# The first bias of an expert layer: added by VectorE instead of by a TensorE product, and the expert number read earlier on TensorE

## The chip, the cores and the metric
The kernel runs on one NeuronCore of a Trainium2 chip. The metric is the device time of one launch in microseconds. The engines are called PE (TensorE), DVE (VectorE), ACT (ScalarE), POOL (GpSimd) and SP (SyncE, which here issues DMAs and waits). The times before are three runs: 1462.31, 1463.79 and 1467.72 us.

## What is computed
Cross attention and then a layer of experts, both with a residual, all in fp32 accuracy:

```python
x = x + xattn(layernorm(x), ctx_768, ...)        # 16 x 224 rows of 512, 16 heads, 750 keys
x = x + ffn(layernorm(x), w1, b1, w2, b2, ...)
# ffn: 8 experts of width 256, the 2 best per row by the router, softmax over the 2
h = gelu(einsum('bsd,edh->bseh', x, w1) + b1)    # exact gelu
expert_out = einsum('bseh,ehd->bsed', h, w2) + b2
out = einsum('bse,bsed->bsd', gates, expert_out)
```

The change concerns `b1`, an array of 8 experts x 256 values, and the register that says which expert a tile of rows belongs to.

## The kernel before
The whole work is one program in which each engine has its own list of instructions, written out by hand, with semaphores between them. Matrix products of fp32 accuracy are made of three products of split operands: x = high + low, w = high + low, and high x high + high x low + low x high.

**Attention** is 64 groups (16 batches, 4 groups of 4 heads), pipelined over five groups. `first`, `second`, `third` and `fourth` of each engine give the order inside a group, and `after(g)` and `before(g)` are hooks between groups. The weights of the experts are loaded by SP in 16 pieces of 512 KB (`load_pieces`) during the last groups. A piece is split by ACT (`w_part`, L1007: high) and then DVE (L1400: low = piece - high). ACT splits 11 pieces in its `after(GROUPS)`, DVE four in its own, ahead of the last two residual additions (L1300), for the first of which PE's last output projection (L388 to L390, second row of products) waits.

**Placing.** DVE then chooses the two best experts of each row, computes gates and for each row its place in a list sorted by expert, padded so that every tile of 128 list entries belongs to one expert. There are 63 tiles (`TILES`). The list goes into `table_x` (rows to gather) and `table_t` (rows to add to), and `which_i[i]` is the expert number of tile i.

**The loop over 63 tiles**, which the change touches. For tile i:
- POOL gathers 128 rows of 516 values into `xg` (L801), six tiles ahead, and adds the finished 128x512 tile to `out` by an indirect DMA (L809).
- PE `fold_x`: four transposes (L2110). ACT `x_high` (L1157) and DVE `x_low` (L1666) make high and low parts of it.
- PE `up`: the bias product L2118 (ones, 128x128, times `b1_hl[:, e, :]`, whose row 0 holds the high part of b1, row 1 the low part, and all others zeros), then 12 products with w1 (L2120 to L2122) of 256 columns each, all into one PSUM tile.
- ACT `gelu` (L1164) from that PSUM tile into `hid`.
- PE `fold_h`: two transposes of `hid` (L2130); ACT `h_high` (L1170), DVE `h_low` (L1671).
- PE `down`: six products of 512 columns with w2 (L2139 to L2141).
- DVE `y_bias` (L1682) adds b2 out of `b2_all`, in which the 8 rows of b2 are spread over all partitions; ACT `y_scale` (L1177) multiplies by the gate.

PE's order in turn i is fold_x(i+2), read of the expert number of i+1 (`expert_of`, L2145), up(i+1), down(i), fold_h(i+1). DVE's is x_low(i+2), y_bias(i), read of the number of i+1 (L1676), h_low(i+1). ACT's is x_high(i+2), gelu(i+1), h_high(i+1), y_scale(i). A read is a load of one value out of SBUF into a register of the engine's sequencer, which other instructions of that engine then use in their addresses.

**How b1 gets to its place before.** b1 comes in as 16 rows of 128 values per lane (`b1_s`), PE transposes it into a PSUM bank (L1918, end of group 63), ACT copies the high part (`b1_th`, L1013), DVE the low part (`b1_tl`, L1405). POOL sets `ones_r` to 1 and `b1_hl` to 0 (L732, L733), then SP moves the two parts into rows 0 and 1 of `b1_hl` with two DMAs (L539, L541). The semaphore `b1_both` tells that both have landed. ACT waits for it ahead of its 11 splits, because both parts lie where weights are written later, and PE ahead of the tile loop.

Of the kernel before, what the change touches and what calls it, by code (L numbers as in the profile page):

```python
# [146 lines left out]
def expert_phase(nc, x1_d, w1, b1, w2, b2, centroids, w_route, ident_d, gates_dram, out):  # L147
    x, ctxT, wqT, bq, wkT, bk, wvT, bv, woT, bo, ident, x1 = SCRATCH["attention"]
    with ExitStack() as es:
# [77 lines left out]
        b1_hl, ones_r = in_a("b1_hl", [P, E, DE], F32R), in_a("ones_r", [P, P], F32R)  # L227
# [22 lines left out]
        b1_th, b1_tl = in_q("b1_th", [2 * E, P], F32R), in_q("b1_tl", [2 * E, P], F32R)  # L250
# [75 lines left out]
        b1_hi, b1_both = sem("b1_hi"), sem("b1_both")  # L326
# [18 lines left out]
        ctxv = ctxT.rearrange("b (c p) n -> b c p n", p=P)  # L345

# [53 lines left out]
        with nc.Block() as block:  # L400

            @block.sync
            def _(sp):
# [126 lines left out]
                def before(g):  # L530
# [5 lines left out]
                    if g == GROUPS:  # L536
                        sp.wait_ge(zeroed, 1)
                        sp.wait_ge(b1_hi, 1)
                        sp.dma_start(b1_hl[0:1, :, :].bitcast(F32), b1_th[:, :].bitcast(F32)).then_inc(b1_both, 16)  # L539
                        wait_free(sp, "b1", 0)  # L540
                        sp.dma_start(b1_hl[1:2, :, :].bitcast(F32), b1_tl[:, :].bitcast(F32)).then_inc(b1_both, 16)  # L541
                        sp.wait_ge(s_full, 12 * GROUPS)
                        load_pieces(E + 2, 2 * E)
# [52 lines left out]
                wait_full(sp, "O1", B - 1)  # L596
                sp.dma_start(b2_all[:, :, :], b2.rearrange("(a e) n -> a e n", a=1).broadcast_to([P, E, D])
# [15 lines left out]
            def _(pool):  # L613
# [110 lines left out]
                def constants():  # L724
# [7 lines left out]
                    pool.memset(ones_r[:, :].bitcast(F32), 1.0).then_inc(made, 1)  # L732
                    pool.memset(b1_hl[:, :, :].bitcast(F32), 0.0).then_inc(zeroed, 1)  # L733

                def after(g):
# [13 lines left out]
                    pool.wait_ge(made, 7)  # L749
# [6 lines left out]
                    pool.wait_ge(made, 11)  # L756
# [57 lines left out]
                pool.wait_ge(zeroed, 3)  # L814
# [17 lines left out]
            def _(act):  # L832
# [176 lines left out]
                def after(g):  # L1009
                    if g == GROUPS - 1:  # L1010
                        wait_full(act, "b1", 0)
                        act.wait_ge(x_full, XU * GROUPS)
                        act.activation(b1_th[:, :], bank_of("b1", 0)[0:2 * E, 0:P], ACT.Copy).then_inc(b1_hi, 1)  # L1013
                    if g == GROUPS:
# [4 lines left out]
                        act.wait_ge(b1_both, 32)  # L1019
# [140 lines left out]
                def gelu(i):  # L1160
                    act.wait_ge(h_full, i + 1)
                    if i >= 2:
                        act.wait_ge(ht_full, i - 1)
                    act.activation(hid[:, i % 2, :], HP[:, i % 2, 0:DE], ACT.Gelu).then_inc(gelu_done, 1)  # L1164
# [30 lines left out]
            def _(dve):  # L1195
# [206 lines left out]
                def after(g):  # L1402
                    if g == GROUPS - 1:
                        dve.wait_ge(b1_hi, 1)
                        dve.tensor_tensor(out=b1_tl[:, :], in0=bank_of("b1", 0)[0:2 * E, 0:P], in1=b1_th[:, :],  # L1405
                                          op=ALU.subtract).then_inc(freed("b1", 0), 1)
# [3 lines left out]
                    if g == GROUPS + 2:  # L1410
                        dve.wait_ge(made, 8)
# [106 lines left out]
                dve.wait_ge(made, 5)  # L1518
# [25 lines left out]
                dve.wait_ge(zeroed, 3)  # L1544
# [15 lines left out]
                dve.wait_ge(made, 8)  # L1560
# [50 lines left out]
                dve.wait_ge(made, 12)  # L1611
# [65 lines left out]

                def y_bias(i, e):
# [21 lines left out]
            @block.tensor  # L1700
            def _(pe):
# [447 lines left out]
                pe.wait_ge(b1_both, 32)  # L2149
# [5 lines left out]
                up(0, e)  # L2155
                fold_h(0)
# [53 lines left out]
```

## Time and profile before
| | before |
|---|---|
| median of 3 runs | 1463.79 us |
| the profiled execution: its own time, its span | 1467.88 us, 1466.0 us |
| mean granted TensorE clock in it | 0.976 of full |
| PE busy | 1389.4 us (95%) |
| DVE busy | 970.8 us (66%) |
| ACT busy | 840.8 us (57%) |
| POOL busy | 1082.7 us (74%) |

All views are of the one profiled execution; its own time and its span differ by what lies around the instructions. "Idle before" of a row is the time in which the engine had nothing under way just before that instruction, and behind the arrow stands what ended it. PEld is PE's weight load, which overlaps products. A name with a q (PEldq) is the engine's sequencer: register work and waits, which are not counted as busy. Ends of PE's products are modelled. A chain of waits gives each microsecond to one instruction: to the one that the end of the span was waiting for.

### The profile page before, as it was taken

How to read it: one execution, taken by the hardware profiler on the slowest of the kernel's cores; microseconds unless marked ns; L12 is line 12 of the kernel's file. 1: busy time of each engine (PE TensorE's matmuls, PEld its weight loads, DVE VectorE, ACT ScalarE, POOL GpSimd, SP SyncE). 2: the span in 40 equal slices, each digit the busy share in tenths (PEclk: the TensorE clock that was granted, in tenths of full speed). 3: DMA queues.
4: the chain of work that ended last, by engine and by line, in shares of the span. 5: the costliest groups of instructions: out<-in, count | busy, mean ns of one | idle time of the engine just before them, and what ended most of it. 6: DMA issues, size and time to landing. Idle time of an engine off the chain costs nothing.

```text
span 1466.0 us, 34315 instructions
## 1 busy us (share of the span) xinstructions
PE 1389.4 (95%) x11524; PEld 1109.4 (76%) x11524; DVE 970.8 (66%) x1429; ACT 840.8 (57%) x1825; POOL 1082.7 (74%) x915
## 2 busy tenths in 40 slices
PE   4899999999999999999999999999999767999997
PEld 4777777787777787777777777777786446999986
DVE  6666767677676767677767676767667476444443
ACT  5546565666656566666665656665664552555554
POOL 3468787878787879797978787887877804776775
PEclk9989999999999999999999999999999687999999
DMA  7354545555454555555555554555454763887785
GB/s 242 90 130 109 166 128 154 149 136 156 124 155 123 161 137 140 140 140 139 142 145 154 134 156 124 167 132 152 118 136 125 243 128 75 146 144 131 144 143 85
DMA packets 134952, 206.74 MB, mean 141 GB/s; under 512 B 33808, under 2 KB 70832, under 8 KB 134656
## 3 DMA queue, kind: packets, MB, share of 16 engines
q1 hardware_dynamic: 120544, 173.20, 43.5%
q0 software_dynamic: 14240, 31.35, 11.9%
q8 instruction: 99, 1.62, 0.5%
q14 instruction: 69, 0.57, 0.1%
HBM read 64.29 MB, written 38.66 MB: 70 GB/s over the span
## 4 chain that ended last, share of the span: by engine, by line
PE 87%; DVE 5%; POOL 2%; issue 2%; DMA 2%; SPq 1%; ACT 1%; POOLq 0%; DVEq 0%; ACTq 0%
PE M L388 13%; PE S L1849 12%; PE M L389 12%; PE M L390 12%; PE O L1865 10%; PE M L1826 5%; PE M L2122 2%; PE M L2121 2%; PE M L2120 2%; PE M L2139 2%; PE M L2140 2%; PE M L2141 2%; PE S L2110 2%; PE M L1883 2%; POOL psum_p L634 1%
## 5 line engine op out<-in xcount | busy, mean ns | idle before, releaser
L634 POOL TENSOR_TENSOR psum_p<-psum_p,pr 125x896 f32<-125x896 f32 x254 | 549.8, 2165 | 107.5 <-ACT pr L917 82.1
L917 ACT ACTIVATE pr<-S 125x448 f32<-125x448 f32 x768 | 386.9, 542 | 205.2 <-PE S L1849 196.5
L1257 DVE TENSOR_REDUCE mx_parts<-M 112x2 f32<-112x1024 f32 x256 | 305.6, 1216 | 84.9 <-PE M L1826 84.8
L1849 PE MATMUL S<-qst,kst 128*125 128x224 f32 x1536 | 268.3, 289 | 5.4 <-ACT pr L917 3.2
L1849 PEld LDWEIGHTS S<-qst,kst 128*125 128x125 f32 x1536 | 223.6, 190 | 53.8 <-issue 22.1
L1865 PE MATMUL O<-pr,v 125*32 125x224 f32 x3072 | 185.4, 364 | 0.1
L1261 DVE TENSOR_REDUCE mx_parts<-M 112x4 f32<-112x952 f32 x128 | 141.0, 1143 | 59.6 <-PE M L1826 59.5
L631 POOL TENSOR_TENSOR psum_p<-pr 125x896 f32<-125x896 f32 x64 | 135.5, 2117 | 32.4 <-ACT pr L917 32.3
L388 PE MATMUL M<-ctx_h,wk_h 128*128 128x376 f32 (+1 forms) x384 | 136.2, 355 | 0.6 <-DVE mx_parts L1257 0.5
L389 PE MATMUL M<-ctx_l,wk_h 128*128 128x376 f32 (+1 forms) x384 | 129.9, 338 | 0.0
L885 ACT ACTIVATE kh_s<-M,bk_s 128x376 fp32r<-128x376 f32 (+1 forms) x128 | 73.1, 571 | 98.5 <-PE M L390 95.8
L390 PE MATMUL M<-ctx_h,wk_l 128*128 128x376 f32 (+1 forms) x384 | 129.3, 337 | 0.0
L809 POOL DMA_INDIRECT out<-y_out,table_t x63 | 99.9, 1585 | 39.0 <-ACT y_out L1177 17.9
L801 POOL DMA_INDIRECT xg<-rows_d,table_x x63 | 64.0, 1016 | 85.9 <-DVE settled L1660 45.8
L1865 PEld LDWEIGHTS O<-pr,v 125*32 125x32 f32 x3072 | 86.7, 111 | 53.6 <-issue 15.4
L1277 DVE RECIPROCAL M<-M 128x224 f32<-128x224 f32 x64 | 100.1, 1564 | 38.5 <-PE M L1883 38.3
L388 PE MATMUL M<-wv_h,ctx_h 128*125 128x512 f32 x288 | 117.1, 407 | 0.0
L390 PE MATMUL M<-wv_h,ctx_l 128*125 128x512 f32 x288 | 113.6, 394 | 0.0
L389 PE MATMUL M<-wv_l,ctx_h 128*125 128x512 f32 x288 | 113.5, 394 | 0.0
L1826 PE MATMUL M<-kh_s,q_own 32*112 32x512 f32 (+1 forms) x1024 | 94.4, 399 | 17.0 <-DVE mx_parts L1257 7.7
L1826 PEld LDWEIGHTS M<-kh_s,q_own 32*112 32x112 f32 x1024 | 41.8, 170 | 62.3 <-issue 48.1
L1245 DVE SCALAR_TENSOR_TENSOR kl_s<-M,bk_s,kh_s 128x376 fp32r<-128x376 f32 (+1 forms) x128 | 76.5, 598 | 16.2 <-ACT kh_s L885 15.8
(259 smaller groups left out, 2999.9 us busy)
## 6 DMA issues: line engine op xcount, KB each, us to landing
kst<-kh_s SPq DMA_DIRECT2D x512, 93.8 KB, 2.2
kst<-kl_s SPq DMA_DIRECT2D x256, 93.8 KB, 2.2
ctx_r<-ctxT SPq DMA_DIRECT2D x48, 375.0 KB, 3.7
qst<-qh_s SPq DMA_DIRECT2D x128, 112.0 KB, 3.0
rows_d<-x_res SPq DMA_DIRECT2D x32, 448.0 KB, 4.7
w_l<-w SPq DMA_DIRECT2D x16, 512.0 KB, 7.7
x_ln<-x SPq DMA_DIRECT2D x17, 448.0 KB, 4.6
q_own<-qh_s SPq DMA_DIRECT2D x256, 28.0 KB, 1.8
```

The source lines that it names most:

```text
L388: pe.matmul(out, lhs[0], rhs[0], start=first, stop=False)
L389: pe.matmul(out, lhs[0], rhs[1], start=False, stop=False)
L390: return pe.matmul(out, lhs[1], rhs[0], start=False, stop=last)
L631: pool.tensor_tensor(out=total, in0=tiles[0], in1=tiles[1], op=ALU.add).then_inc(sum_step, 1)
L634: pool.tensor_tensor(out=total, in0=total, in1=tiles[half], op=ALU.add).then_inc(sum_step, 1)
L917: act.activation(pr[0:KP, (3 * g + p) % 2, j, :, :], S[0:KP, n % SB, 0:2 * NQ].rearrange("p (i n) -> p i n", i=2), ACT.Exp).then_inc(exp_d ...
L1257: dve.tensor_reduce(mx_parts[0:QP, pair, u, 0:1], M[0:QP, pair, 0:FIRST_KEYS], AX.X, ALU.max).then_inc(max_done, 1)
L1261: dve.tensor_reduce(mx_parts[0:QP, pair, :, 1], both, AX.X, ALU.max).then_inc(max_done, 1)
L1277: dve.reciprocal(den, den).then_inc(inverted, 1)
L1826: last = pe.matmul(M[0:QP, j, at:at + w], q_own[head, g % 2, QP * qt:QP * (qt + 1)], kh_s[head, g % 2, off:off + w], start=True, stop=True)
L1849: last = pe.matmul(S[0:KP, n % SB, NQ * h:NQ * (h + 1)], kst[:, i, j, o:o + KP], qst[:, i, j, :], start=True, stop=True)
L1865: last = pe.matmul(O[HD * j:HD * (j + 1), 0:NQ], v[0:KP, 2 * p + i, HD * j:HD * (j + 1)], pr[0:KP, (3 * g + p) % 2, j, i, :], start=(p == ...
```

## The change
1. **The bias.** `b1_hl` and `ones_r` go, `b1_all` (128 x 8 x 256, fp32) comes. ACT copies the transposed b1 whole into `b1_t`; SP writes it to DRAM (`b1_rows`, 8 KB, in the place of two DMAs of 8 KB) and reads it back spread over all 128 partitions (`b1_line`, 1 MB) ahead of the load of `b2_all`. POOL's two memsets go, as do DVE's low part, ACT's wait for `b1_both` ahead of its splits and PE's ahead of the loop.
2. **The loop.** PE's product L2118 goes. DVE adds the bias: `h_bias(i)` reads the PSUM tile and `b1_all[:, e, :]` and writes `hid`. The gelu works in place in `hid`. DVE's order in turn i becomes read of the number of i+1, h_bias(i+1), x_low(i+2), y_bias(i), h_low(i+1). up(i) waits for `biased` of i-2 instead of the gelu of i-2.
3. **The read on PE.** The number of tile i+2 is read behind down(i), ahead of fold_h(i+1); before, that of i+1 was read between fold_x(i+2) and up(i+1).

```diff
@@ SP
                     if g == GROUPS:
-                        sp.wait_ge(zeroed, 1)
-                        sp.wait_ge(b1_hi, 1)
-                        sp.dma_start(b1_hl[0:1, :, :].bitcast(F32), b1_th[:, :].bitcast(F32)).then_inc(b1_both, 16)
                         wait_free(sp, "b1", 0)
-                        sp.dma_start(b1_hl[1:2, :, :].bitcast(F32), b1_tl[:, :].bitcast(F32)).then_inc(b1_both, 16)
+                        sp.dma_start(b1_rows, b1_t[:, :]).then_inc(b1_sent, 16)
                         sp.wait_ge(s_full, 12 * GROUPS)
                         load_pieces(E + 2, 2 * E)
...
                 wait_full(sp, "O1", B - 1)
+                sp.wait_ge(b1_sent, 16)
+                sp.dma_start(b1_all[:, :, :].rearrange("p e f -> p (e f)"),
+                             b1_line.broadcast_to([P, E * DE])).then_inc(b1_in, 16)
@@ POOL
-                    pool.memset(ones_r[:, :].bitcast(F32), 1.0).then_inc(made, 1)
-                    pool.memset(b1_hl[:, :, :].bitcast(F32), 0.0).then_inc(zeroed, 1)
@@ ACT
-                        act.activation(b1_th[:, :], bank_of("b1", 0)[0:2 * E, 0:P], ACT.Copy).then_inc(b1_hi, 1)
+                        act.activation(b1_t[:, :], bank_of("b1", 0)[0:2 * E, 0:P], ACT.Copy).then_inc(freed("b1", 0), 1)
...
-                        act.wait_ge(b1_both, 32)
                         for n in range(ACT_EARLY):
                             w_part(n)
...
                 def gelu(i):
-                    act.wait_ge(h_full, i + 1)
-                    if i >= 2:
-                        act.wait_ge(ht_full, i - 1)
-                    act.activation(hid[:, i % 2, :], HP[:, i % 2, 0:DE], ACT.Gelu).then_inc(gelu_done, 1)
+                    act.wait_ge(biased, i + 1)
+                    act.activation(hid[:, i % 2, :], hid[:, i % 2, :], ACT.Gelu).then_inc(gelu_done, 1)
@@ DVE
-                    if g == GROUPS - 1:
-                        dve.wait_ge(b1_hi, 1)
-                        dve.tensor_tensor(out=b1_tl[:, :], in0=bank_of("b1", 0)[0:2 * E, 0:P], in1=b1_th[:, :],
-                                          op=ALU.subtract).then_inc(freed("b1", 0), 1)
...
+                def h_bias(i, e):
+                    dve.wait_ge(h_full, i + 1)
+                    if i >= 2:
+                        dve.wait_ge(ht_full, i - 1)
+                    dve.tensor_tensor(out=hid[:, i % 2, :], in0=HP[:, i % 2, 0:DE], in1=b1_all[:, e, :],
+                                      op=ALU.add).then_inc(biased, 1)
...
                 x_low(0)
                 e = expert_of(0)
                 x_low(1)
+                dve.wait_ge(b1_in, 16)
+                h_bias(0, e)
                 h_low(0)
                 dve.wait_ge(b2_in, 16)
                 for i in range(TILES):
+                    if i + 1 < TILES:
+                        after = expert_of(i + 1)
+                        h_bias(i + 1, after)
                     if i + 2 < TILES:
                         x_low(i + 2)
                     y_bias(i, e)
                     if i + 1 < TILES:
-                        e = expert_of(i + 1)
                         h_low(i + 1)
+                        e = after
@@ PE
                     if i >= 2:
-                        pe.wait_ge(gelu_done, i - 1)
+                        pe.wait_ge(biased, i - 1)
                     h = HP[:, i % 2, 0:DE]
-                    pe.matmul(h, ones_r[:, :], b1_hl[:, e, :], start=True, stop=False)
                     for c in range(DC):
-                        pe.matmul(h, xTs[:, 0, i % 2, c, :], w1_h[:, e, c, :], start=False, stop=False)
+                        pe.matmul(h, xTs[:, 0, i % 2, c, :], w1_h[:, e, c, :], start=c == 0, stop=False)
...
-                pe.wait_ge(b1_both, 32)
...
                 up(0, e)
+                after = expert_of(1)
                 fold_h(0)
                 pe.wait_ge(ew_lo, DVE_LOW)
                 for i in range(TILES):
                     if i + 2 < TILES:
                         fold_x(i + 2)
                     if i + 1 < TILES:
-                        after = expert_of(i + 1)
                         up(i + 1, after)
                     down(i, e)
+                    if i + 2 < TILES:
+                        later_one = expert_of(i + 2)
                     if i + 1 < TILES:
                         fold_h(i + 1)
                         e = after
+                    if i + 2 < TILES:
+                        after = later_one
```

## Rows read from the trace of the kernel before
**Rows 1.** The page's first line: the span of the profiled execution.
```profile
span 1466.0 us, 34315 instructions
```
**Rows 2.** Windows, 1240 to 1440 us: PE, PEld, DVE, ACT, POOL busy, clock, DMA share, GB/s.
```profile
1240.00:1440.00 200.00, 199.73 (x1376) 181.08 (x1375) 98.18 (x166) 108.67 (x221) 139.97 (x109) 1.00 0.77 138
```
**Rows 3.** Chain of waits, 1300 to 1315 us: shares, then start us, us, what.
```profile
by line: PE M L2121 13.6%; PE M L2120 13.5%; PE M L2122 12.9%; PE M L2139 12.5%; PE M L2140 12.4%; PE M L2141 12.4%; PE S L2110 11.6%; PE M L2118 5.7%; PE O L2130 2.9%; PE M L2130 2.9%; issue 0.1%
...
1303.15 0.44 PE S L2110 x4
...
1306.76 0.44 PE S L2110 x4
1307.19 0.12 PE M L2118
```
**Rows 4.** Timeline of PE and PEld in one tile: start us, us, engine, line, operation.
```profile
1308.47 0.29 PE L2122 MATMUL M<-w_h,xTs 128*128 x1
...
1309.75 0.40 PE L2141 MATMUL M<-w_h,hTs 128*128 x1
1309.76 0.37 PEld L2130 LDWEIGHTS O<-id_s,hid 128*128 128x128 f32 x2
1309.99 0.38 PE L2130 MATMUL O<-id_s,hid 128*128 128x128 f32 x2
```
**Rows 5.** Timeline of DVE and ACT in the same tile, idle time before in brackets.
```profile
1307.41 0.72 ACT L1177 ACTIVATE y_out<-y_raw,xg 128x512 f32<-128x512 f32 x1 [0.23 <-DVE y_raw L1682]
1307.62 0.43 DVE L1671 TENSOR_TENSOR hTs<-M,hTs 128x256 fp32r<-128x256 f32 x1 [0.24 <-issue]
...
1308.04 0.58 ACT L1157 ACTIVATE xTs<-S 128x512 fp32r<-128x512 f32 x1
...
1308.65 0.69 DVE L1666 TENSOR_TENSOR xTs<-S,xTs 128x512 fp32r<-128x512 f32 x1 [0.60 <-ACT xTs L1157]
1308.80 0.38 ACT L1164 ACTIVATE hid<-M 128x256 f32<-128x256 f32 x1 [0.18 <-PE M L2122]
...
1310.30 0.69 DVE L1682 TENSOR_TENSOR y_raw<-M,b_all 128x512 f32<-128x512 f32 x1 [0.96 <-PE M L2141]
```
**Rows 6.** Timeline at two places where PE restarts: the first tile, the last.
```profile
1229.32 0.38 ACT L1164 ACTIVATE hid<-M 128x256 f32<-128x256 f32 x1 [1.09 <-PE M L2122]
1229.75 0.29 PEld L2130 LDWEIGHTS O<-id_s,hid 128*128 128x128 f32 x2 [0.77 <-ACT hid L1164]
...
1456.81 0.19 PEld L2139 LDWEIGHTS M<-w_h,hTs 128*128 128x128 f32 x1 [1.35 <-issue]
1456.84 0.47 PE L2139 MATMUL M<-w_h,hTs 128*128 x1 [1.14 <-DVE hTs L1671]
```
**Rows 7.** By source: PE's register read (ns min/median/max), and L2118's idle (us, times).
```profile
L2145 PEldq TENSOR_LOAD <-which_i x63: 298/307/969, 1225.2 to 1451.3; - x63
L2145 PEldq FUSED_REGOPS  x63: 151/151/165, 1225.7 to 1451.8; - x63
...
  issue: 1.7, 6
```
**Rows 8.** Chain of waits and timeline at the start of the expert phase.
```profile
1164.48 4.11 DMA b_hl<-b_tl
...
1166.24 0.34 ACT L946 ACTIVATE lg_parts<-M 128x224 f32<-128x224 f32 x1
1168.77 10.53 ACT L1007 ACTIVATE w_h<-w_l 128x1024 fp32r<-128x1024 f32 x11 [2.20 <-DMA b_hl<-b_tl]
...
1169.86 4.69 DVE L1400 TENSOR_TENSOR w_l<-w_l,w_h 128x1024 fp32r<-128x1024 f32 x4 [1.81 <-ACT w_h L1007]
...
1175.21 0.48 PE L388 MATMUL M<-wo_h,oT_h 128*112 128x512 f32 x1 [2.70 <-DVE x_ln L1300]
```
**Rows 9.** Windows after it, columns as in rows 2.
```profile
1172.80:1176.20 3.40, 0.99 (x4) 0.80 (x5) 3.30 (x5) 3.40 (x4) 0.75 (x2) 1.00 0.89 321
1176.20:1179.60 3.40, 3.40 (x9) 2.12 (x7) 0.88 (x1) 3.10 (x4) 0.00 (x0) 0.50 0.00 0
```

More of the change, by code:

```diff
@@ L226, in expert_phase @@
         w1_h, w1_l = in_a("w1_h", [P, E, DC, DE], F32R), in_a("w1_l", [P, E, DC, DE], F32R)
-        b1_hl, ones_r = in_a("b1_hl", [P, E, DE], F32R), in_a("ones_r", [P, P], F32R)
+        b1_all = in_a("b1_all", [P, E, DE])
         b1_s, lane = in_a("b1_s", [P, 2 * E]), in_a("lane", [P, 1])
@@ L249, in expert_phase @@
         in_q, end_q = region(q_own_at)
-        b1_th, b1_tl = in_q("b1_th", [2 * E, P], F32R), in_q("b1_tl", [2 * E, P], F32R)
+        b1_t = in_q("b1_t", [2 * E, P])
         assert end_q[0] <= q_own_at + 2 * NQ * 4
@@ L325, in expert_phase @@
         made, zeroed, masks = sem("made"), sem("zeroed"), sem("masks")
-        b1_hi, b1_both = sem("b1_hi"), sem("b1_both")
+        b1_sent, b1_in = sem("b1_sent"), sem("b1_in")
+        biased = sem("biased")
         gate_out, need_done, safe = sem("gate_out"), sem("need_done"), sem("safe")
@@ L345, in expert_phase @@
         ctxv = ctxT.rearrange("b (c p) n -> b c p n", p=P)
+        b1_rows = gates_dram.rearrange("a b c -> (a b c)")[0:E * DE].rearrange("(r c) -> r c", c=P)
+        b1_line = gates_dram.rearrange("a b c -> (a b c)")[0:E * DE].rearrange("(a n) -> a n", a=1)
         raw_k = pr[:].rearrange("p a b c n -> p (a b c n)")[:, 0:CC * D]
@@ L748, in after @@
                     pool.memset(going[:, :, :], 1.0).then_inc(made, 1)
-                    pool.wait_ge(made, 7)
+                    pool.wait_ge(made, 6)
                     pool.memset(going[:, :, 0:1], 0.0).then_inc(made, 1)
@@ L755, in after @@
                     pool.tensor_scalar(upper_half[:, :], token[:, :], 0.0, None, ALU.is_ge).then_inc(made, 1)
-                    pool.wait_ge(made, 11)
+                    pool.wait_ge(made, 10)
                     pool.tensor_tensor(out=token16[:, :], in0=token[:, :], in1=upper_half[:, :], op=ALU.add).then_inc(made, 1)
@@ L812, in add_rows @@
                                             oob_is_err=False, compute_op=ALU.add).then_inc(added[i % YO], 16)
-                pool.wait_ge(zeroed, 3)
+                pool.wait_ge(zeroed, 2)
                 for n in range(YO):
@@ L1410, in after @@
                     if g == GROUPS + 2:
-                        dve.wait_ge(made, 8)
+                        dve.wait_ge(made, 7)
                         dve.tensor_scalar(behind[:, :], iota[:, :], float(DUMP + 1), lane[:, 0:1], ALU.add,
@@ L1517, in _ @@
                 gp, g1, g2 = gap[0:QP, :], gate4[0:QP, :, 0, 0], gate4[0:QP, :, 1, 0]
-                dve.wait_ge(made, 5)
+                dve.wait_ge(made, 4)
                 wait_free(dve, "lg", B - 1)
@@ L1543, in _ @@
                 dve.wait_ge(gap_exp, 1)
-                dve.wait_ge(zeroed, 3)
+                dve.wait_ge(zeroed, 2)
                 dve.wait_ge(x1_out, 16 * B)
@@ L1559, in _ @@
                 dve.wait_ge(sums_full, 1)
-                dve.wait_ge(made, 8)
+                dve.wait_ge(made, 7)
                 dve.tensor_tensor_scan(runs.rearrange("p e k -> p (e k)"), going[0:QP].rearrange("p e k -> p (e k)"), sums,
@@ L1609, in find_rows @@
                                       op=ALU.is_equal).then_inc(row_done, 1)
-                dve.wait_ge(made, 12)
+                dve.wait_ge(made, 11)
                 dve.wait_ge(xn_out, 32 * B)
```

## The prediction
> **What bounds the kernel now.** I read the page first, for the span of the profiled execution [rows 1], then the last fifth of it, where the changed loop runs, with the view of windows. From 1240 to 1440 us PE is busy 199.73 of 200 us at full granted clock (2.4 GHz), while DVE works 98, ACT 109 and POOL 140 us [rows 2]. The chain of waits says the same more sharply: over four tiles it consists of PE instructions and 0.1% of "issue", and one tile takes 1306.76 - 1303.15 = 3.61 us [rows 3]. So in this stage every 0.1 us that PE's instruction stream loses or gains in a tile is worth 62 times as much. The stage before it, the start of the expert phase, is a chain through several engines. There I looked for what the old bias path holds up, and found ACT waiting for a DMA of it [rows 8].
>
> **1. The bias product goes.** In the chain L2118 stands with 0.12 us per tile [rows 3]. Its own row would say 0.36 us, but most of that lies under its neighbours. There are 63. The first runs before the loop is filled, at half clock, and is dealt with in step 2. The other 62 give 62 x 0.12 = 7.4 us.
>
> **2. DVE adds the bias between the up products and the gelu.** The nearest row for the new add is the DVE subtraction of the same 128x256 elements, one operand in PSUM: 0.43 us. Its start follows the pattern of y_bias, which has the same two waits and an address from a register: 0.15 us after PE's last product ends (1309.75 + 0.40 = 1310.15, start 1310.30) [rows 4, 5]. Then come a hand-over to ACT of 0.04 us (as x_high ending at 1308.62 and x_low starting at 1308.65), the gelu, 0.38 us, and 0.05 us from the gelu to PE's weight load (1229.70 to 1229.75) [rows 5, 6]. From the end of the up products to the load of fold_h this makes 0.15 + 0.43 + 0.04 + 0.38 + 0.05 = 1.05 us, where today it is 0.04 + 0.38 and then 0.58 us in hand.
>
> The cover is down(i), which lies between them. The up products end at 1308.47 + 0.29 = 1308.76 and the load of fold_h starts at 1309.76, 1.00 us later [rows 4]. That is when PE has it start, not when it must. On a free PE at the end of the kernel a load starts at 1456.81 and its product ends at 1457.31, 0.50 us later for 512 columns. 128 columns take 0.13 us less (0.40 against 0.38 - 0.11 for the first of two), so 0.37 us [rows 4, 6]. fold_h's first product now ends at 1309.99 + 0.27 = 1310.26, so its load could start at 1309.89, 1.13 us after the up products. The bounds for the wait are 0 (1.05 against 1.13) and 0.10 us a tile (1.05 and 0.05 for a slower gelu, against 1.00). I take 0, as the restart on a free PE is the nearest row; the other end costs 62 x 0.10 = 6.2 us.
>
> The gelu now reads SBUF, not PSUM. ACT's 128x512 from SBUF, with a scale from a tensor, takes 0.72 us against 0.58 us from PSUM [rows 5]; part of this is the scale, so 0.05 us is my bound for a slower gelu. The Trainium skill ("VectorE: DVE Perf Modes", "The TRN2 errata") gives ScalarE 224 fixed cycles for an SBUF source and 172 for PSUM; at its 1.2 GHz this would be 0.04 us against the change, still inside the 0.08 us in hand. No row here isolates it.
>
> On DVE, x_low now stands behind the new add: it would start at 1308.76 - 0.12 + 0.15 + 0.43 + 0.03 = 1309.25 and end at 1309.94 [rows 4, 5]. The next up products start about 0.65 us (six transposes of 0.11) behind 1309.64, at 1310.3; 0.35 us are in hand. y_bias, next on DVE, needs it at 1310.18. ACT does nothing new. DVE goes from 1.8 to 2.2 us of work per 3.5 us. For the first tile nothing covers the add: +0.58 us (0.15 + 0.43), against its product at half clock, at least 2 x 0.12 = 0.24 us. I take +0.3 us.
>
> **3. PE reads the expert number earlier.** The register load takes 307 ns in the median and up to 969 ns, followed by 0.15 us of register work; by the program's order the sequencer reaches it only behind fold_h's wait for the gelu. Where it was slow PE stood still ahead of L2118: 1.7 us in 6 tiles [rows 7]. Behind down(i) the read runs beside the up and down products, while the sequencer would wait for the gelu anyway: it has at least the 1.05 us of step 2. At the old place the gelu, 0.58 us later now (0.15 + 0.43 + 0.04, against 0.04), would put the read that much closer to the up products in every tile. Gain 1.7 us; bounds 0 and 1.7.
> Here the Trainium skill speaks against the change: "TensorE: Matmul & The Clock Gate" (Spec table) gives PE a queue of 64, and "Perfetto Trace Analysis" (Tensor Engine Instruction) has the sequencer go on while an instruction waits in the queue. By that rule the read would run far ahead already, and moving it be worth 0. The rows are against it: six stalls of 0.3 us end at L2118 with "issue".
> DVE's read moves the other way, from behind y_bias to behind h_low, where it runs in DVE's idle time ahead of h_full, beside the up products; it costs nothing, and h_low loses a wait.
>
> **4. The old bias path at the start of the expert phase.** ACT is ready for its 11 splits of weights when keep_parts ends, 1166.24 + 0.34 = 1166.58, and stands still for 2.20 us more for the DMA of b1_tl, which lands 4.11 us after its issue. DVE stands still 1.81 us for the first split, then does four of its own until 1174.55, then the residual for which PE waits 2.70 us at 1175.21 [rows 8]. From there on the chain runs through PE, DVE and ACT without a cover to the table and the first gather. Without the wait ACT starts 2.2 us earlier. DVE is free 1.8 us earlier, so the chain gains 1.8 us. Bounds: 0 if another wait stands there, and 1.8 + 1.7. The latter is clock: PE's second row of products, from 1175.21, ran its first microsecond at full (2.4 GHz) and the rest, 3.4 us of it, at half clock (1.2 GHz) [rows 9]; started at 1173.4, most of it would lie in the full stretch and take half of 3.4 us. That stretch is not tied to the kernel, so I take no gain from it, and it can also go against me.
> The added DMAs on SP: 8 KB out, in place of two of 8 KB in, ahead of six weight loads, which can start earlier, as SP no longer waits for POOL's memset; and 1 MB in, ahead of b2 and the gates. At 321 GB/s [rows 9] that is 3.3 us more for the gates. Their cover is DVE's placing of the tokens, from the gates to the table, which the first gather waits for too; without it, 3.3 us. POOL loses two memsets, and nobody waits for what stands behind them.
>
> **Sum.** 7.4 + 1.7 + 1.8 - 0.3 = 10.6 us. In the loop POOL's queue catches up more slowly after each change of expert (its work of 140 / 200 x 3.61 = 2.5 us per tile [rows 2] meets 3.5, not 3.6), for which I take off 0.3 us: 10.3 us. The profiled execution took 1467.9 us (span 1466.0 [rows 1]), 4.1 us above the median of 1463.8; it would come out at 1457.6. The median goes to 1463.8 - 10.3 = **1453.5**, -0.70%. A measurement of this kernel can tell about 0.5% (7.3 us) from no change.
>
> **Rivals.**
> *fold_h waits for the gelu* (20%). If the load must start at its present place, PE waits 0.05 to 0.10 us per tile: 3 to 6 us are given back: 1456.5 to 1459.7. For it: 1.05 us is more than 1.00. Against: the restart row.
> *Slower* (4%). The same place, or x_low behind the add, but much later: it decides from 10.3 / 62 = 0.17 us of wait per tile. With the add as long as y_bias, 0.69 us [rows 5], the chain of step 2 is 1.31 us; against 1.00 us that is 0.31 us a tile, 19.2 us, and 1472.7. Against it: the row of 256 elements is 0.43 us, from PSUM too.
> *The bias path at the start is hidden anyway* (13%): another wait holds ACT or DVE at 1166 to 1169. Then 1453.5 + 1.8 = 1455.3.
> *Reading ahead is worth nothing* (8%): the stalls come from code loading, and stay. Then 1453.5 + 1.7 = 1455.2. The rule on the queue would give this too.
> *Forecast* 55%.
>
> **Numbers.** The range takes in the clock at the start (1.7 us down) and 2 us for the median of few runs; upwards the first rival: 1449 to 1460. Faster by over 0.5% is below 1456.5: the forecast but for 3 points, both small rivals, a fifth of the first: 0.74; same 0.22; slower 0.04.
>
> **What would show it.** L2118's group is gone and the chain's period per tile is 3.49 us; idle before fold_h's load stays near 0 (if it says "<-ACT hid" with 0.05 us or more, the first rival holds); a DVE group hid<-M,b1_all of 63, mean near 425 ns; gelu at 385 to 430 ns. No stall with "issue" ahead of the up products. ACT's first split starts near 1166.6 with no DMA ahead of it, and the first gather near 1217.5. Wrong would be: a period of 3.55 or more, or a first gather that doesn't move.

## The result, and the profile after

The changed kernel takes 1455.45 us in the median of 5 runs (1453.5 to 1458.86), beside 1463.79 us for the kernel before: ratio 0.9939, 95% interval 0.9925 to 0.9952, or 8.3 us less. Two later comparisons, on two different chips, gave 0.9956 and 0.9942. The forecast was 10.3 us less and 1453.5 us. The profiled execution took 1458.86 us, 3.4 us above its median, as the one of before stood 4.1 us above its own.

The page's first lines, of after:
```profile
span 1456.8 us, 34248 instructions
...
PE 1378.8 (95%) x11461; PEld 1100.2 (76%) x11461; DVE 988.9 (68%) x1491; ACT 843.2 (58%) x1825; POOL 1085.0 (74%) x913
```
The same window as in [rows 2], of after (PE, PEld, DVE, ACT, POOL busy, clock, DMA share, GB/s):
```profile
1240.00:1440.00 200.00, 199.47 (x1375) 180.84 (x1374) 117.16 (x230) 114.88 (x229) 146.35 (x114) 1.00 0.79 145
```
PE is as full as it was, and fewer of its instructions are spent on a tile: the chain of waits, 1303 to 1311 us, to be read against [rows 3], has a tile every 3.48 us (1306.99 - 1303.51, 1310.47 - 1306.99) in place of 3.61, with no product of L2118 and no share of "issue".
```profile
1303.51 0.44 PE S L2117 x4
...
1306.99 0.44 PE S L2117 x4
...
1310.47 0.44 PE S L2117 x4
```
One tile's timeline of after, against [rows 4, 5] (idle time before in brackets):
```profile
1308.58 0.28 PE L2128 MATMUL M<-w_h,xTs 128*128 x1
...
1309.00 0.42 DVE L1677 TENSOR_TENSOR hid<-M,b_all 128x256 f32<-128x256 f32 x1 [1.06 <-PE M L2128]
...
1309.34 0.68 DVE L1661 TENSOR_TENSOR xTs<-S,xTs 128x512 fp32r<-128x512 f32 x1
...
1309.46 0.42 ACT L1163 ACTIVATE hid<-hid 128x256 f32<-128x256 f32 x1 [0.60 <-DVE hid L1677]
...
1309.85 0.40 PE L2147 MATMUL M<-w_h,hTs 128*128 x1
1309.93 0.30 PEld L2136 LDWEIGHTS M<-id_s,hid 128*128 128x128 f32 x2
1310.09 0.38 PE L2136 MATMUL M<-id_s,hid 128*128 128x128 f32 x2
```
The up products end at 1308.86, the add starts 0.14 us later, the gelu ends at 1309.88, and the weight load of fold_h starts at 1309.93, 1.07 us behind the up products. That is 0.07 us later than in [rows 4], and yet its product starts 0.24 us behind the last down product, as that one did behind its own predecessor (0.23), so without a gap. The interval of 1.07 us is the same in every tile, to 0.01 us (1.15 in the first), so the load now starts when the gelu is done, and the product when PE is free. The groups by line say it for all 63 tiles (busy us, mean ns, idle time before); fold_h writes to `O` and `M` in turn, so it has two groups:
```profile
L1677 DVE TENSOR_TENSOR hid<-M,b_all 128x256 f32<-128x256 f32 x63 | 26.8, 425 | 68.8 <-PE M L2128 68.8
L1163 ACT ACTIVATE hid<-hid 128x256 f32<-128x256 f32 x63 | 26.4, 419 | 41.4 <-DVE hid L1677 41.4
L2136 PE MATMUL O<-id_s,hid 128*128 128x128 f32 x64 | 12.5, 277 | 1.1 <-ACT hid L1163 1.1
L2136 PE MATMUL M<-id_s,hid 128*128 128x128 f32 x62 | 11.8, 272 | 0.0
```
PE's idle time before fold_h all lies at the first tile (1.15 us in its timeline); in the running loop there is none.

The time between four marks in the two profiled executions, us:
```
                                                before    after
start to the first gather's issue              1219.30  1217.42   -1.9
first gather's issue to the end of fold_x(4)     19.03    20.39   +1.4
end of fold_x(4) to the end of fold_x(62)       210.87   202.61   -8.3
end of fold_x(62) to the end of the span         16.84    16.38   -0.5
```
So the running loop gives the gain, and its start takes some of it back. How much of the first row belongs to the change, the experiments tell.

### The profile page after: what moved, and what is told of

It is laid out like the page before. It is cut to its first block, busy times and chain, and to the rows that moved or that the text cites. A ratio compares the mean times of both kernels' runs of the same rounds, so it can differ in the third digit from the quotient of the medians.

```text
span 1456.8 us, 34248 instructions
## 1 busy us (share of the span) xinstructions
PE 1378.8 (95%) x11461; PEld 1100.2 (76%) x11461; DVE 988.9 (68%) x1491; ACT 843.2 (58%) x1825; POOL 1085.0 (74%) x913
## 4 chain that ended last, share of the span: by engine, by line
PE 84%; DVE 6%; POOL 3%; SPq 2%; issue 2%; DMA 2%; ACT 1%; POOLq 0%; DVEq 0%; ACTq 0%
PE M L392 13%; PE M L393 12%; PE M L394 12%; PE S L1856 12%; PE O L1872 10%; PE M L1833 5%; PE M L2126 2%; PE M L2128 2%; PE M L2127 2%; PE M L2145 2%; PE M L2147 2%; PE M L2146 2%; PE S L2117 2%; PE M L1890 2%; POOL psum_p L638 2%
## 5 line engine op out<-in xcount | busy, mean ns | idle before, releaser
L811 POOL DMA_INDIRECT out<-y_out,table_t x63 | 99.9, 1585 | 38.5 <-ACT y_out L1176 18.7
L803 POOL DMA_INDIRECT xg<-rows_d,table_x x63 | 64.0, 1017 | 74.1 <-DVE settled L1655 40.8
```

## The experiments

Ratios are to the kernel before in the same series, on the same chip; each series had its own chip. The kernel before took 1467.45, 1464.23 and 1464.29 us in the three series.

### First series: the parts one by one

**The bias product put back** (the changed kernel, with one more product a tile; the next one, with start=True, overwrites its result):
```diff
                     for c in range(DC):
+                    pe.matmul(h, xTs[:, 0, i % 2, 0, :], w1_h[:, e, 0, :], start=True, stop=True)
```
(it stands ahead of the loop over c)


> The changed kernel with a 256-column product more at the head of each up, where the bias product stood; the next one starts the sum anew, so its result is not used. If PE's instruction stream is the bound of the loop, the product costs its issue interval, 0.12 us in each of 62 tiles: period 3.60 us, 7.4 us on top of 1455.5, 1462.9. If the loop is by now bound by the chain through DVE and ACT (1.07 us beside the down products), part of it is hidden: the first up products of a tile would start earlier relative to fold_h and the period would stay below 3.55 us, at most +4 us.


Measured: 1465.88 us, ratio 0.9984 (0.9974 to 0.9995). Against the 0.9939 of the whole change, which was measured in another comparison, this is about 6.6 us. The price fits, but the trace had something that neither trace of before and after had. Its timeline at one tile, PE, DVE, ACT and POOL:
```profile
1266.72 1.59 POOL L811 DMA_INDIRECT out<-y_out,table_t  x1 [0.30 <-issue]
...
1267.12 0.28 PE L2129 MATMUL M<-w_h,xTs 128*128 x1
...
1268.43 0.42 DVE L1677 TENSOR_TENSOR hid<-M,b_all 128x256 f32<-128x256 f32 x1 [2.07 <-PE M L2129]
...
1268.89 0.42 ACT L1163 ACTIVATE hid<-hid 128x256 f32<-128x256 f32 x1 [1.61 <-DVE hid L1677]
...
1269.36 0.33 PE L2137 MATMUL M<-id_s,hid 128*128 128x128 f32 x1 [0.57 <-ACT hid L1163]
```
The last up product ends at 1267.40, and DVE starts the add 1.03 us later, where 0.14 us is the rule. The semaphore events of the trace put PE's signal at 1268.30, 0.90 us behind the product's end; DVE's own register read was done by 1267.0. Seven such late signals (0.53 to 0.95 us) stand in this execution, each followed by a tile that took 0.44 to 0.85 us too long; the traces of before and after have none. The trace also shows what ran beside them: all seven products ended while POOL's instruction that adds a finished tile to `out` (L811, 1.59 us) was running, and all seven signals came 0.01 to 0.09 us before its end, here at 1268.30 against 1268.31.

**The read put back** behind fold_h, all else as in the changed kernel:
```diff
                 up(0, e)
-                after = expert_of(1)
                 fold_h(0)
...
+                        after = expert_of(i + 1)
                         up(i + 1, after)
                     down(i, e)
-                    if i + 2 < TILES:
-                        later_one = expert_of(i + 2)
...
-                    if i + 2 < TILES:
-                        after = later_one
```


> The changed kernel with PE's read of the expert number back between fold_x and up. My theory: PE's sequencer does not pass fold_h before the gelu is done (1309.88 in a tile of the changed kernel's trace), the read then takes 0.2 + 0.30 + 0.15 us and the register work for the first address 0.1 us more, so the first up load starts at about 1310.95 instead of 1310.64: 0.3 us of idle time with issue ahead of L2126's load in every tile, and all of the excess of slow reads comes on top. 62 x 0.3 = 19 us and some 4 us for slow reads: 1475 to 1480. The rival (the sequencer runs far ahead of the queue, the read's place is worth nothing): 1455.5, period 3.48 us.


Measured: 1479.38 us (two runs), ratio 1.0075 (1.0051 to 1.0099): 17 to 20 us more than the changed kernel by its three ratios, and slower than the kernel before. The view by source of the first up product's line says where:
```profile
L2126 PEldq FUSED_REGOPS  x252: 46/46/46, 1224.3 to 1466.6; - x126
...
  issue: 24.8, 74
```
(idle time of the weight loads and of the products added up) and the timeline of PEld shows it at three tiles in a row:
```profile
1303.82 0.19 PEld L2126 LDWEIGHTS M<-w_h,xTs 128*128 128x128 f32 x1 [0.25 <-issue]
...
1307.71 0.19 PEld L2126 LDWEIGHTS M<-w_h,xTs 128*128 128x128 f32 x1 [0.37 <-issue]
...
1311.49 0.19 PEld L2126 LDWEIGHTS M<-w_h,xTs 128*128 128x128 f32 x1 [0.27 <-issue]
```
The sequencer's read doesn't get past fold_h while that waits for the gelu: here, as in the kernel before, it starts 0.17 to 0.33 us behind the gelu's end in nearly every tile. The gelu now ends about 0.6 us later, the register load (301 ns in the median here) starts only then, and in these three tiles no weight load runs for 0.25 to 0.37 us; a tile takes 3.79 us in the median, not 3.48. The rival that the read's place is worth nothing is out. The read had to move because the add was put in.

**The read moved alone**, in the kernel before:
```diff
+                after = expert_of(1)
                 fold_h(0)
...
-                        after = expert_of(i + 1)
                         up(i + 1, after)
                     down(i, e)
+                    if i + 2 < TILES:
+                        later_one = expert_of(i + 2)
...
+                    if i + 2 < TILES:
+                        after = later_one
```


> The kernel before with nothing but PE's read moved behind down. My theory: the six to eight stalls ahead of L2118 (1.7 us in its trace) go and the period stays 3.60 us; 1463.8 - 1.8 = 1462.0. The rival: the stalls are code loading or the like and stay, with issue, ahead of L2118 or elsewhere, 1463.8.


Measured: 1462.15 us, ratio 0.9964 (0.9953 to 0.9976): 5.3 us less, three times what I had put on it. Its trace has 13 late signals, and yet no tile of the loop took 0.3 us more than the median of 3.61.

**ACT's wait for the bias moved alone**, in the kernel before, from ahead of its 11 splits of weights to behind the first eight:
```diff
-                        act.wait_ge(b1_both, 32)
                         for n in range(ACT_EARLY):
+                            if n == E:
+                                act.wait_ge(b1_both, 32)
                             w_part(n)
```


> The kernel before, in which ACT waits for the two DMAs of the bias parts only ahead of the ninth of its splits (the first that writes a w2 piece), not ahead of the first. My theory: the first split starts at the end of keep_parts, near 1166.6 where it was 1168.8, with no DMA named ahead of it, DVE's first split 1.8 us earlier, and the first gather 1.8 us earlier if the output projection of the last batch runs at the same clock (1.7 us either way where it does not): 1462.0. The rival: something else holds the chain there (the first row of the projection, the landing of a piece), and the first gather stays within 0.5 us of 1219.3: 1463.8.


Measured: 1467.33 us, ratio 0.9992 (0.9982 to 1.0002): 1.2 us less, anything from 2.6 less to 0.3 more, so neither the theory's 1.8 nor the rival's 0 is excluded. In its trace ACT's first split follows keep_parts without a wait, 1.03 us before the DMA of b1_tl lands. Its loop is that of the kernel before, and its window from 1240 to 1440 us has PE busy 198.07 us, 1.7 us less than [rows 2], with eight late signals of 0.44 to 1.04 us in the trace. On this chip the kernel before was 3.7 us slower in the median than in the first comparison. Taken together, the parts came to 6.6 + 5.3 + 1.2 = 13.1 us against 8.3 for the whole, so either the add costs some 4 to 5 us that no trace shows, or the parts were measured where signals come late. Two more series went to that.

### Second series: the whole again, the order on DVE, the start, the gathers

**The changed kernel again.**


> The changed kernel once more, beside the kernel before on the chip of this series. The earlier series gave, on a chip where the kernel before took 1467.45 us, about 6.6 us for the second bias product (against the 0.9939 of the first comparison), 5.3 us for the read moved alone and 1.2 us for the late wait alone: 13.1 us in parts, against 8.9 us for the whole. Theory A, the parts were sized against another session and the whole is steady: ratio 0.993 to 0.995 here too. Theory B, the whole is worth its parts where the kernel before has more late signals (its trace there showed stalls of 0.4 to 1 us at some eight tiles): ratio 0.990 to 0.992. In the trace: period 3.48 us, the loop start at half clock until some 11 us after the first gather, at most one stall of 0.75 us.


Measured: 1457.1 us, ratio 0.9956 (0.9941 to 0.9971), just above theory A's 0.993 to 0.995, which its interval reaches, and wholly above theory B's 0.990 to 0.992. In this trace the loop has no stall at all: fold_x(4) to fold_x(62) takes 201.87 us, 58 tiles of 3.48.

**x_low ahead of the add** on DVE:
```diff
+                    if i + 2 < TILES:
+                        x_low(i + 2)
                     if i + 1 < TILES:
                         after = expert_of(i + 1)
                         h_bias(i + 1, after)
-                    if i + 2 < TILES:
-                        x_low(i + 2)
```


> VectorE's x_low of the tile two further on goes ahead of the new bias add instead of behind it. Theory: the chain add, gelu, load of fold_h has 0.05 us or less in hand, and x_low (0.68 us, whose input ScalarE finishes about when up ends) pushes the add back by some 0.6 us; part of it comes back because the late tile gives ScalarE its input later too, and I expect +0.27 us a tile, period about 3.75 us, +17 us in all (ratio to the changed kernel about 1.012, to the kernel before about 1.006), with PE's idle time before fold_h put down to ACT. Rival: the load of fold_h is not the bound and the order on VectorE is worth nothing: period 3.48 us.


Measured: 1486.2 us (two runs), ratio 1.015 (1.0128 to 1.0171), 29.1 us more than after_again: the theory's sign and place, but nearly twice its size. The waits from 1240 to 1440 us (us in total, times, longest):
```profile
PEld O L2136 <- ACT hid L1163: 19.6, 25, 1.2
PEld M L2136 <- ACT hid L1163: 18.6, 25, 1.4
DVE hid L1677 <- issue: 18.3, 38, 1.1
```
The first two say that fold_h waits for the gelu in every tile. The shortest tiles take 3.74 us, as worked out. What I had missed is the third: with the add late, DVE's own register read stands right ahead of it. It takes 490 ns in the median here and up to 968, and whatever it takes beyond 0.3 us goes into the tile, as at 1304.95:
```profile
1304.95 0.42 DVE L1677 TENSOR_TENSOR hid<-M,b_all 128x256 f32<-128x256 f32 x1 [0.75 <-issue]
...
1305.41 0.42 ACT L1163 ACTIVATE hid<-hid 128x256 f32<-128x256 f32 x1 [1.93 <-DVE hid L1677]
```
In the changed kernel the same read took up to 1051 ns and nobody waited, since DVE is idle for 1.06 us before the add. The order of two adjacent lines is worth over three times the change.

**PE kept at work ahead of the first gathered tile:**
```diff
+                pe.wait_ge(rest_out, PE_LOW)
+                for n in range(WARM):
+                    pe.matmul(Y[:, 0, :], w1_h[:, 0, 0, 0:P], w1_h[:, 0, 0:2, :], start=True, stop=True)
                 pe.wait_ge(which_done, 1)
                 pe.wait_ge(table_done, 1)
-                pe.wait_ge(rest_out, PE_LOW)
```
with WARM = 20; the results are not used.


> The changed kernel with 20 products of 128x512 on PE in the 7.9 us that it sat idle ahead of the first gathered tile, results unused. Theory: the changed kernel loses some 1.2 us against the kernel before, and 3 to 4 us against what it could have, because the first four stages of the expert loop run at a granted clock of 0.50 (up(0) and up(1) take 2.7 us each where 1.5 us is the time at 1.00, the first fold 1.09 where 0.60 is). With PE busy until the gather lands, the clock is 1.00 from there on: up(0) and up(1) 1.5 us each, and 3 to 4 us less than the changed kernel (ratio to it about 0.9975). Rival: the gaps of 1 to 2 us between the first stages bring the clock down again or it does not rise at all: nothing gained, or up to 0.8 us lost where the products run past the landing.


Measured: 1455.14 us, ratio 0.9938 (0.9922 to 0.9954), 2.0 us below after_again, with intervals that overlap. The trace is clearer: from the first gather's issue to the end of fold_x(4) it is 18.65 us against 20.47. The windows show that half of the theory came true:
```profile
1216.00:1218.00 2.00, 0.62 (x4) 0.39 (x4) 1.59 (x2) 0.60 (x1) 1.84 (x1) 1.00 0.52 132
1218.00:1222.00 4.00, 3.80 (x16) 3.27 (x16) 0.80 (x2) 1.88 (x2) 2.84 (x3) 0.57 0.64 172
```
The first fold ran at 1.00 (0.63 us for four transposes, 1.09 in after); then PE waited 1.46 us for the second tile, the clock went to 0.50, and up(0) took 2.8 us, most of it at half clock all the same. up(1) ran at full.

**Seven gathered tiles in flight**, XG = 7 instead of 6:


> The changed kernel with seven gathered tiles in flight instead of six. Theory: the changed loop is 3.48 us a tile and POOL's issues fall behind at each change of expert; a gather that takes 7.0 us then comes 0.75 us too late at tile 46 of the changed kernel's trace, and there are none or one such stall a run: 0 to 1 us less than the changed kernel. Rival: more in flight lengthens each gather or holds up the scatters, and the time is the same or 0.5 us more.


Measured: 1454.86 us, ratio 0.9938 (0.9916 to 0.9959), not to be told from the whole. What PE waited for ahead of fold_x from 1235 to 1450 us, by source, in after:
```profile
L2117 PE MATMUL S<-id_s,xg x236: 271/273/328, 1237.2 to 1440.1; 128*128 128x128 f32 x118
...
  DMA xg<-rows_d,table_x: 1.3, 2
```
(two rows, weight load and product, of one stall of 0.75 us at tile 46, whose gather took 7.03 us). With seven in flight this row is absent; with six it was absent in after_again too, and 2.7 us in two rows (one stall of 1.45 us) in the third execution below.

### Third series: do the parts add up?

> The changed kernel a third time, as the control of this series: 0.9939 and 0.9956 of the kernel before so far, so 0.993 to 0.997 here, 6 to 10 us. It decides with the next two whether the parts add up: in the first series they were measured without the whole beside them.


Measured: 1455.93 us, ratio 0.9942 (0.9929 to 0.9955).


> The changed kernel with the bias product left on PE once more a tile, on zero rows, beside the whole change on one chip. Theory A, the parts add up and the gap came from comparing two series (in the trace of product_twice seven signals of up's last product reached VectorE 0.5 to 0.9 us late and cost 0.6 to 0.75 us each, in the traces of the changed kernel none did): the period is 3.60 against 3.48 us, so 7.4 us above after_third, which makes it -1 us or nothing against the kernel before; with such late signals up to 4 us more. Theory B, the whole is less than its parts because the added chain costs about 4 us somewhere: 6 us or less above after_third.


(The added product is the one shown above, of a tile with its weights; "zero rows" is a slip.) Measured: 1463.2 us, ratio 0.999 (0.9977 to 1.0003): 7.3 us above after_third, as this text's theory A has it, and good to 2 to 3 us by the two intervals. The trace has no late signal and no stall:
```profile
1240.00:1440.00 200.00, 200.00 (x1389) 182.20 (x1388) 113.57 (x222) 111.75 (x223) 141.98 (x112) 1.00 0.78 141
```


> The kernel before with PE's register read moved alone, beside the whole change. On record for the first time was -1.8 us, measured -5.3. Theory A, the first profile of the kernel before happened to have few slow reads and the real worth is 3 to 5 us: -3 to -5 us again, and product plus read comes to more than the whole by some 3 us. Theory B, the 5.3 us were of that chip: -1 to -3 us here, and product, read and wait together give the whole within 1.5 us.


Measured: 1463.35 us, ratio 0.9992 (0.9982 to 1.0002): 0.9 us less, anything from 2.6 less to 0.3 more. No late signal in its trace. This is nearest to this text's theory B: 7.3 for the product, 0.9 for the read and 1.2 for the wait, less the 1.4 us that the loop's start loses (below), are 8.0 us, and the whole is 8.4 on this chip, with each figure good to 1 to 3 us. No hidden cost of the add is needed, though one of 2 us would not be seen. The 5.3 us belonged to a chip on which signals came late; there the loop of read_moved_alone took 209.79 us from fold_x(4) to fold_x(62) and that of late_wait_alone, with the read in the old place, 215.26. So the place of the read matters more where something else is late too. These two traces agree with that, with 13 late signals in the one and 8 in the other; why that chip's signals were late isn't shown.

> The changed kernel with seven tiles in flight and PE kept at work through its waits at the start of the expert loop: 26 unused products of 128x512 ahead of the first fold, 6 between the first two folds, 3 behind up(0). In the trace of warm_start (20 products ahead alone) the clock was 1.00 when the first tile came and fell to 0.50 in the 1.5 us wait for the second, so that up(0) took 2.7 us; from the first gather to the end of the fifth fold it took 18.65 us against 20.39 and 20.47 in the changed kernel. Theory: with the waits filled up(0) takes 1.5 us and the stretch 17.0 us, 3.4 us less than the changed kernel, and no tile waits for its gather: ratio to the kernel before about 0.992, 3 to 4 us below after_third. Rival: the filling products run past what they wait for or the clock falls all the same: as warm_start or worse.


The edit, beside XG = 7, where `warm(n)` issues n of the unused products shown above, and the three names stand for 26, 6 and 3:
```diff
+                pe.wait_ge(rest_out, PE_LOW)
+                warm(WARM)
                 pe.wait_ge(which_done, 1)
                 pe.wait_ge(table_done, 1)
-                pe.wait_ge(rest_out, PE_LOW)
                 fold_x(0)
+                warm(BETWEEN)
                 fold_x(1)
...
                 after = expert_of(1)
+                warm(BEHIND)
                 fold_h(0)
```
Measured: 1452.29 us, ratio 0.9913 (0.9897 to 0.9929), 12.0 us less than the kernel before and 3.6 less than after_third. PE at the loop's start, of warm_filled:
```profile
1219.10 0.60 PE L2118 MATMUL S<-id_s,xg 128*128 128x128 f32 x4
1219.45 1.64 PE L2156 MATMUL M<-w_h 128*128 128x512 f32 x6
1220.93 0.60 PE L2118 MATMUL S<-id_s,xg 128*128 128x128 f32 x4
...
1223.22 0.95 PE L2156 MATMUL M<-w_h 128*128 128x512 f32 x3
1224.52 0.44 PE L2137 MATMUL O<-id_s,hid 128*128 128x128 f32 x2 [0.35 <-ACT hid L1164]
```
and the windows from 1216 us on, all at 1.00:
```profile
1216.00:1220.00 4.00, 4.00 (x21) 3.27 (x20) 3.69 (x4) 0.20 (x1) 3.39 (x3) 1.00 0.48 128
1220.00:1224.00 4.00, 3.83 (x24) 3.03 (x22) 1.78 (x3) 2.27 (x3) 3.09 (x4) 1.00 0.56 146
```
From the first gather's issue to fold_x(4) it takes 17.48 us (17.0 expected; 20.58 in after_third), and the loop runs without a stall, 201.70 us (203.27 in after_third, which had one stall for a gather). By these two traces the filled waits are worth 3.1 us and the missing stall 1.6 us. This version beats both kernels.

## Why the prediction was right, and where not

The direction, the place and the main term were right, and the measured time, 1455.45, lies 2.0 us above the 1453.5 forecast and inside the range. Point by point:

**Step 1, the product, 7.4 us: right.** Period 3.61 to 3.48 us; measured by itself 7.3 us, good to 2 to 3. Reading 0.12 us off the chain and not 0.36 us off the row was the step that made the forecast.

**Step 2, the added chain, wait 0: right in the loop, mis-sized at the first tile.** 1.05 us forecast from the up products to the load of fold_h, 1.07 measured. The load's start before was not a limit, as the restart row had it: it moved by 0.07 us and PE had no gap. x_low behind the add ends at 1310.02 and the next up product starts at 1310.66, so the 0.35 us in hand were no less. The gelu from SBUF takes 419 ns for 385, 34 ns more. The Trainium skill ("VectorE: DVE Perf Modes", "The TRN2 errata") led to 0.04 us, and the rows agree. The slower rival needed an add of 0.69 us; it took 425 ns.
The first tile was put at +0.3 us. In the traces with the add the stretch from the first gather's issue to fold_x(4) takes 20.39 to 20.87 us in seven executions (after, after_again, after_third, seven_gathers, read_old_place and the two of product_twice), and without it 18.77 to 19.03 in four: 1.4 to 2.1 us more. At half clock the old bias product had cost 0.43 us there (1226.29 to 1226.72 in the chain of before), so the fold was late by 0.46 us only; the rest is clock. PE's wait for the first gelu grew from 0.5 to 1.15 us, and the granted clock came back to 1.00 only at 1232.16, 9.0 us behind the second fold's start, where before it was 5.7 us. up(1) ran whole at half clock:
```profile
1226.00:1230.00 4.00, 2.85 (x14) 2.56 (x14) 0.85 (x2) 1.23 (x4) 0.79 (x1) 0.50 0.50 156
1230.00:1234.00 4.00, 4.00 (x22) 3.69 (x22) 1.21 (x3) 0.83 (x3) 0.00 (x0) 0.73 0.02 4
```
In the kernel before the second window has 0.90. I had priced the wait and not what the clock does behind it.

**Step 3, the read, 1.7 us: of the right size as far as can be told, and too small a claim.** By itself 0.9 us (2.6 less to 0.3 more) on a chip without late signals, and no stall with "issue" is left ahead of the up products but 0.2 us, once. What made the slow reads was left open. The traces show a thing beside them that neither the forecast nor its rival of code loading has: POOL's gather (L801 or L803, 0.99 us in the loop). In the kernel before 57 of the reads of PE and DVE from 1230 us on overlap one, and 32 of these took over 0.4 us; of the other 66, 3 did. What the gather does to a read was not tried. And the forecast's remark that the old place "would put the read that much closer" was worth 17 to 20 us, which I had not worked out. The rival that reading ahead is worth nothing is refuted for the changed kernel, and with it, for a read that stands behind a waiting instruction, the rule on the queue: the Trainium skill ("TensorE: Matmul & The Clock Gate", Spec table; "Perfetto Trace Analysis", Tensor Engine Instruction) would have the read run ahead, and the rows of read_old_place show it held behind fold_h's wait. Where page and rows differ, the rows decide.

**Step 4, the head, 1.8 us: mis-sized by what the traces show**, though the forecast's mark (first gather near 1217.5) was met by 1217.42. What does not hold in general is the sentence "Without the wait ACT starts 2.2 us earlier". The wait of 2.20 us in [rows 8] was due to one DMA that took 4.11 us in that execution. In two other executions of the same path, read_moved_alone and read_moved_again, it took 2.2 and 2.7 us:
```profile
1165.17 5.79 ACT L1007 ACTIVATE w_h<-w_l 128x1024 fp32r<-128x1024 f32 x6 [0.29 <-DMA b_hl<-b_tl]
```
```profile
1166.30 0.34 ACT L946 ACTIVATE lg_parts<-M 128x224 f32<-128x224 f32 x1
1166.76 3.90 ACT L1007 ACTIVATE w_h<-w_l 128x1024 fp32r<-128x1024 f32 x4
```
ACT waited 0.29 us in the one and next to nothing in the other. From keep_parts (the start of L946) to the first gather it was 49.6 and 50.3 us in these two, with the old path; 49.4 to 50.4 in the executions of the changed kernel; and 53.1 in the one that the forecast was read from. So the added DMAs cost nothing that shows, and by these traces the head is worth about 0 to 0.3 us outside that one execution, not 1.8. In late_wait_alone, where the DMA landed 1.03 us behind the start of ACT's splits, it took 50.7 us; that run's own time, 1.2 us less (2.6 less to 0.3 more), decides between neither. The third rival's price, none for the head, fits, and its 1455.3 us is near what was measured, but not by its mechanism: no other wait held ACT, the DMA had mostly landed in time. That its time is met is chance, as the other terms were off too.

**The catch-up of POOL, 0.3 us: mis-sized.** One gather too late in two of three executions with six in flight, 0.75 and 1.45 us, none in two with seven.

The forecast's terms with what they measured: product 7.3 for 7.4; stalls of the read 0.9 (-0.3 to 2.6) for 1.7; head 0 to 0.3 by the traces, 1.2 by its run, for 1.8; loop start -1.4 for -0.3; gathers -0.7 in the mean of three for -0.3. They sum to 6.3 us, 7.3 with the run's value for the head, up to 8 with the upper end for the read; the three comparisons gave 8.3, 6.4 (0.0044 x 1464) and 8.4 us, each good to 2 us. So the mechanism of the loop was right, and the four smaller terms were put too favourably, by 0.4 to 1.5 us each in their middle values; the measured gain, 2 us below the forecast, says the same.

One sum in the forecast is wrong in itself: 52 points of the forecast, 13 and 8 of the small rivals and a fifth of 20 make 0.77 for "faster by over 0.5%", and not 0.74.

## What to carry to other kernels

Before work is put on another engine between two PE stages, find the latest moment at which the next stage must load, from a place where PE restarts freely, and not the moment at which it loads today: here an estimate of 0.08 us in hand, beside 1.05, carried 62 tiles. A register read in the order of a waiting engine belongs to the critical chain as soon as what it waits behind gets later. A wait for a DMA seen once in one execution is one draw of its duration: look at the same wait in a second trace before it enters a sum, and price a longer wait of PE together with the clock behind it. Where an engine's small operations are slow now and then, look at what every other engine is doing at those moments before calling it noise.

## What the runs showed of the hardware

- A signal of PE can come 0.25 to 1.1 us after the product has ended: 7 to 13 times in three of the four executions on one chip (three times in the fourth), not once in the ten other executions. All 31 of these products ended while POOL's indirect DMA instruction of L809 (L811 in the changed kernel; 1.59 us) was running, and 29 of the signals came within 0.11 us of its end. In the other ten executions 39 to 55% of the products with a signal also end inside that instruction, and none is late, so the meeting alone does not make a signal late. The traces of that chip also lack 29 to 39 of PE's roughly 245 signals in the loop, the others none. POOL's spans are rough, and no run was aimed at this: the cause is open.
- A register load from SBUF takes 0.30 us as a rule and up to 1.05 us on PE and DVE alike. In all 14 executions taken together, from 1230 us on, 506 reads overlap a POOL gather instruction, and 350 of them took over 0.4 us; of the 1189 others, 56 did. In x_low_first, where the median of DVE's reads was 490 ns against 311 ns in after, the slow ones mostly began 0.2 to 0.5 us ahead of such a gather. This is a coincidence in time that no run took apart.
- Products whose results nobody reads made the loop's start 3.1 us faster (17.48 for 20.58 us): in warm_start the granted clock was 1.00 before the wait of 1.46 us for the second tile and 0.50 behind it, and up(0) then took 2.8 us; in warm_filled, without that wait, it stayed at 1.00 and up(0) took 1.7.
